# First attention: the subtraction of the row maximum moved from GpSimd to VectorE, with five neighbours moved to other places

## The chip, the core and the metric

The kernel runs on one core of one Trainium2 chip. The metric is the device time of one execution in microseconds (us); it is told as the median of three runs.

## The reference, cut to what matters

Sixteen images of 16 x 16 pixels with 128 channels go through three layers, each with a residual sum:

- `x = x + conv(group_norm(x))`: the first attention, windows of 8 x 8 pixels, 16 heads of 32, with a relative position bias and shift masks: `attn = softmax(q k^T * scale + bias + mask)`, `out = attn v`, then an output product;
- `t = t + attention(layer_norm(t))`: the second attention, in the kernel over the 256 tokens of an image, 8 heads of 16;
- `t = t + ffn(layer_norm(t))`: a router picks 2 of 8 experts for each token, and each expert is a gated two-layer net.

The change touches the first attention's softmax, which the kernel computes in explicit passes over scores in SBUF: bias added, maximum of each row, **maximum subtracted**, exponential, sum, reciprocal, product with the reciprocal. The change keeps these passes and what each computes.

## The kernel before, in words

The five engines run separate programs that meet at semaphores; the order of each program is written out by hand. After a prologue comes a loop of 24 iterations, `pipeline` (L366), in which iteration i works on nine images at nine stages of the chain at once (`LAGS`, L361; in the code X, G, A, M, Bm, T, R, L, K):

- X normalises image i+2 (GpSimd: `xns`, `xnl`), G makes its q, k, v for image i+1 (TensorE into `pG`, ScalarE evicts);
- **A** is the first attention of image i, in four units u = 0 to 3 of 128 x 512 scores (`pa`);
- **M** is image i-1: the first attention's output product (L1337, into `pM`), residual sum `t1` (VectorE L945), layer norm statistics (L949, L983, L986), the power -0.5 on GpSimd (`rs1`, L594), the normalised `tn1` (VectorE L1002), its transposes on TensorE (L1363), the split `t1h`/`t1l`, the q and k products of the second attention (L1184 to L1186 into `pM`), their evictions `kst` and `qst` (ScalarE L717, L721; low parts on VectorE L970, L972), and 12 DMAs on SP's queue that lay them out (L457, L461);
- **Bm** and **T** are the second attention of images i-2 and i-3: scores in `pSA`/`pSB` (L1240), their maximum `mxb` (VectorE L979), transposed scores (L1275), exponentials `ptb` (ScalarE L760);
- R, L, K are images i-4 to i-6: second layer norm, router, slots, and the scattering of token records to HBM by indirect DMA from GpSimd's queue (`depart`, `scatter`, L533 to L551).

Every engine runs through eight steps n = 0 to 7 per iteration, and at each step does its share of every stage in a fixed order; an instruction that waits holds everything behind it on its engine. What matters around the change:

- TensorE computes the scores of two units at a time at n = 0 and n = 4 (L1264): the even unit in `pSA`, the odd one in `pTA`. VectorE adds the bias into `pa` (L994, both units, at n = 0 and 4).
- VectorE takes the maximum `mxa` of unit n/2 at n = 0, 2, 4, 6 (L1017); GpSimd subtracts it at the same n (L623); ScalarE takes the exponential of unit (n-1)/2 at n = 1, 3, 5, 7 (L754); VectorE sums it (L1027) and takes the reciprocal `rca` (L1037); GpSimd multiplies (L631, "norm" below) at the same odd n. TensorE transposes the unit one step later (L1349, at n = 2, 4, 6 and the next n = 0), and ScalarE evicts it (`pta`, L777).
- At n = 2 TensorE's product L1337 waits for VectorE's `place` (L925) and `lg` (L899), which use the same bank `pM`.
- TensorE's L1184 for the key, query and value chunks (`pG`) waits until ScalarE has evicted the chunk before (k L687, q L692, v L737), because there is one bank for them.
- At n = 4 VectorE's order is: maximum of the second attention's head (L979), bias adds (L994), `tn1` (L1002), `tn2` (L1009), `mxa` (L1017). At n = 6 it is: `kst`, `qst` low parts (L970, L972), L979, `mxa`.
- GpSimd's order at n = 2 to 5 is: subtract u = 1 and a scatter (n = 2); `rs2` power L601, `mine` L605, two scatters, norm u = 1 (n = 3); `rs1` power L594, subtract u = 2, `xnl` L645, a scatter (n = 4); `t1b` L598, norm u = 2 (n = 5).

After the loop the experts' weights are loaded, tokens are gathered by expert, and the FFN runs (from about 540 us on in the trace); the change does not touch that part.

Of the kernel before, what the change touches and what calls it, by code (L numbers as in the profile page):

```python
# [11 lines left out]
WIN = 64  # L12
# [24 lines left out]
AU, BU = 4, 8  # L37
# [4 lines left out]
TB = 4  # L42
# [19 lines left out]
def wait(eng, sem, value):  # L62

    if value <= 0:
        return
    eng.wait_ge(sem, value)
# [60 lines left out]
def hybrid_kernel(nc, x_tok, x_ch, w0, wo0, bo0, pos, mask, ident_d, gmat_d, sel_d, iota_d,  # L127
# [5 lines left out]
    with ctx:  # L133
# [366 lines left out]
        def _(pool):  # L500
# [52 lines left out]
            def iteration(X, G, A, M, Bm, T, R, L, K):  # L553
# [30 lines left out]
                for n in range(8):  # L584
# [7 lines left out]
                    if n == 4 and M is not None:  # L592
                        pool.wait_ge(m_eps, M.j + 1)
                        pool.tensor_tensor(rs1[:, :], rs1[:, :], half[:, 0:2], ALU.pow).then_inc(m_pow, 1)  # L594
                    if n == 5 and M is not None:
                        pool.wait_ge(m_t, M.j + 1)
                        wait(pool, r_t, M.j - TB + 1)
                        pool.tensor_tensor(t1b[:, M.j % TB, :, :], t1[:, :, :], bo1s[:, :, :], ALU.add).then_inc(m_tb, 1)  # L598
# [13 lines left out]
                    if n == 3:  # L612
                        depart(K, n)
# [5 lines left out]
                    if A is not None and n % 2 == 0:  # L619

                        u = n // 2
                        pool.wait_ge(sa_max, A.j * AU + (u + 1))
                        pool.tensor_tensor(pa[:, u, :, :], pa[:, u, :, :],  # L623
                                           mxa[:, u % 2, :].unsqueeze(2).to_broadcast([128, 8, WIN]),
                                           ALU.subtract).then_inc(sa_sub, 1)
# [28 lines left out]
                    if n != 3:  # L654
                        depart(K, n)
# [186 lines left out]
        def _(v):  # L842
# [47 lines left out]
            def iteration(X, G, A, M, Bm, T, R, L, K):  # L890
                for n in range(8):
# [66 lines left out]
                    if T is not None and n == 7:  # L958
# [7 lines left out]
                                        rco[:, :, :].unsqueeze(3).to_broadcast([128, 2, H1, D1]), ALU.mult).then_inc(ot_nrm, 1)  # L966
                    if M is not None and n == 6:
# [6 lines left out]
                    if M is not None and n == 3:  # L974
                        v.wait_ge(m_st, M.j + 1)
                    if Bm is not None:
                        bank = (pSB, pSA)[n % 2]
                        v.wait_ge(sb_mm, Bm.j * BU + (n + 1))
                        v.tensor_reduce(mxb[:, Bm.par, n % 2, n // 2 * 2:n // 2 * 2 + 2], bank[:, :].rearrange("p (a k) -> p a k", a=2), AX.X,  # L979
                                        ALU.max, negate=True).then_inc(sb_max, 1)  # L980
# [577 lines left out]
```

## Time and profile before

| what | value |
|---|---|
| runs of the kernel before | 706.55, 712.59, 710.5 us; median 710.5 us |
| the profiled execution's own time | 709.77 us |
| its span, first to last instruction | 708.0 us |
| mean granted TensorE clock | 0.954 of full speed |
| busy: PE, PEld, DVE, ACT, POOL | 598.8, 479.6, 438.5, 410.4, 396.2 us |

PE is TensorE's products, PEld its weight loads (they overlap the products), DVE is VectorE, ACT is ScalarE, POOL is GpSimd, SP the engine that only issues DMAs here. "[0.83 <-POOL pa L631]" behind an instruction means that its engine sat idle for 0.83 us in front of it and that the last thing it waited for was GpSimd's instruction of line 631. The profiled execution is one of its own; its time stands 0.7 us under the median of the three runs.

### The profile page before, as it was taken

What the parts mean: (1) busy time and instruction counts of PE and PEld (TensorE: products, weight loads), DVE (VectorE), ACT (ScalarE), POOL (GpSimd) and SP (SyncE); (2) the same over time, 40 slices, a digit from 0 to 9 for tenths busy, and PEclk for the clock granted to TensorE, in tenths of its full rate; (3) what the DMA queues carried; (4) which work ended last, traced back from release to release, by engine and by line L of the source; (5) the groups of instructions that cost most, each with busy time, mean ns of one, the idle gap of its engine ahead of it and who ended that gap; (6) DMA issues with size and microseconds to landing.
All of it is one profiled execution on the core that took longest, in us unless ns stands there. A gap on an engine that the chain in (4) does not pass through costs nothing.

```text
span 708.0 us, 18292 instructions
## 1 busy us (share of the span) xinstructions
PE 598.8 (85%) x6460; PEld 479.6 (68%) x6460; DVE 438.5 (62%) x1325; ACT 410.4 (58%) x915; POOL 396.2 (56%) x503
## 2 busy tenths in 40 slices
PE   4877889999989899899899998988975799999910
PEld 3656667777767777677677776766655688888810
DVE  5534666767767677677776777765433365555625
ACT  2445576787676667766767677444411366666600
POOL 5665653454546576665665765642376066666643
PEclk9799999999999999999999999999996899999975
DMA  7100220231422414224133242243841122233237
GB/s 213 25 2 1 54 54 13 50 69 56 120 43 91 118 37 119 57 86 126 42 104 89 66 122 57 85 124 91 270 182 49 47 87 87 84 91 91 72 135 254
DMA packets 54511, 63.08 MB, mean 89 GB/s; under 512 B 12978, under 2 KB 47794, under 8 KB 53906
## 3 DMA queue, kind: packets, MB, share of 16 engines
q1 hardware_dynamic: 48294, 49.59, 25.3%
q0 software_dynamic: 4544, 9.38, 3.9%
q10 hardware_dynamic: 1584, 2.95, 1.2%
q8 instruction: 53, 0.87, 0.5%
q14 instruction: 36, 0.29, 0.1%
HBM read 35.74 MB, written 28.64 MB: 91 GB/s over the span
## 4 chain that ended last, share of the span: by engine, by line
PE 42%; POOL 17%; issue 15%; DVE 10%; ACT 7%; DMA 6%; SPq 2%; ACTq 0%; DVEq 0%; POOLq 0%
POOL slots L549 5%; POOL pa L623 4%; POOL pa L631 3%; PE pG L1192 3%; PE pSA L1264 3%; DMA slots<-sel_dram 2%; PE pSB L1438 2%; PE pTA L1438 2%; PE pTB L1438 2%; PE pSA L1438 2%; PE pTA L1349 2%; DVE pa L994 2%; PE pOA L1449 2%; PE pOB L1449 2%; PE pOB L1293 2%
## 5 line engine op out<-in xcount | busy, mean ns | idle before, releaser
L623 POOL TENSOR_TENSOR pa<-pa,mxa 128x512 f32<-128x512 f32 x64 | 66.7, 1042 | 110.9 <-DVE mxa L1017 110.8
L664 POOL DMA_INDIRECT ysl<-yo,dst x78 | 75.5, 968 | 59.7 <-DVE yo L1154 45.3
L631 POOL TENSOR_TENSOR pa<-pa,rca 128x512 f32<-128x512 f32 x64 | 67.0, 1047 | 63.5 <-DVE rca L1037 63.3
L760 ACT ACTIVATE ptb<-pTB 128x512 f32<-128x512 f32 x128 | 76.6, 599 | 43.1 <-PE pTB L1275 42.7
L549 POOL DMA_INDIRECT slots<-rec,slot x64 | 65.1, 1017 | 15.9 <-issue 13.2
L777 ACT ACTIVATE pta<-pTA 128x512 f32<-128x512 f32 x64 | 38.5, 602 | 56.1 <-PE pTA L1349 55.6
L1027 DVE TENSOR_REDUCE sma<-pa 128x8 f32<-128x512 f32 x64 | 43.8, 684 | 37.8 <-ACT pa L754 37.8
L754 ACT ACTIVATE pa<-pa 128x512 f32<-128x512 f32 x64 | 40.2, 628 | 42.2 <-POOL pa L623 41.9
L1349 PE MATMUL pTA<-ident,pa 128*128 128x128 f32 x256 | 40.3, 281 | 24.0 <-DVE pa L994 14.7
L979 DVE TENSOR_REDUCE mxb<-pSA 128x2 f32<-128x512 f32 x64 | 44.0, 688 | 25.1 <-PE pSA L1240 24.5
L1275 PE MATMUL pTB<-q,kbd 100*128 100x256 f32 x256 | 56.1, 301 | 0.1
L979 DVE TENSOR_REDUCE mxb<-pSB 128x2 f32<-128x512 f32 x64 | 44.0, 687 | 18.3 <-PE pSB L1240 16.2
L1184 PE MATMUL pG<-xnh,w0h 128*128 128x256 f32 x120 | 40.1, 334 | 13.8 <-ACT v L737 4.8
L1128 DVE COPY xs<-pG 128x256 f32<-128x256 f32 x39 | 16.6, 425 | 55.1 <-PE pG L1431 55.1
L1349 PEld LDWEIGHTS pTA<-ident,pa 128*128 128x128 f32 x256 | 28.0, 142 | 33.2 <-POOL pa L631 19.6
L737 ACT ACTIVATE v<-pG 64x256 f32<-64x256 f32 x120 | 45.3, 378 | 8.8 <-PE pG L1186 7.8
L1275 PEld LDWEIGHTS pTB<-q,kbd 100*128 100x128 f32 x256 | 42.3, 190 | 8.0 <-ACT q L780 2.7
L1314 PEld LDWEIGHTS pOA<-pta,v 128*64 128x64 f32 x1024 | 35.1, 137 | 17.7 <-issue 7.0
L1314 PE MATMUL pOA<-pta,v 128*64 128x64 f32 x1024 | 43.9, 228 | 1.7 <-ACT pta L777 1.1
L1017 DVE TENSOR_REDUCE mxa<-pa 128x8 f32<-128x512 f32 x64 | 43.2, 675 | 0.0
L807 ACT ACTIVATE ws<-fw 128x773 f32 x39 | 33.0, 848 | 17.1 <-issue 10.6
L1264 PEld LDWEIGHTS pSA<-k,q 32*64 32x64 f32 x1024 | 33.1, 135 | 11.7 <-issue 11.7
(227 smaller groups left out, 1738.3 us busy)
## 6 DMA issues: line engine op xcount, KB each, us to landing
slots<-sel_dram SPq DMA_DIRECT2D x16, 1040.0 KB
kbd<-kst SPq DMA_DIRECT2D x128, 48.0 KB, 2.2
q<-qst SPq DMA_DIRECT2D x64, 96.0 KB, 2.2
xt<-slots SPq DMA_DIRECT2D x39, 130.0 KB, 2.2
xch<-x_ch_dram SPq DMA_DIRECT2D x4, 512.0 KB, 5.8
xt<-x_tok_dram SPq DMA_DIRECT2D x16, 128.0 KB, 2.3
xch<-t SPq DMA_DIRECT2D x16, 128.0 KB, 4.6
fw<-f_dram SPq DMA_DIRECT2D x1, 2048.0 KB
```

The source lines that it names most:

```text
L549: pool.indirect_dma_start(slots, bass.IndirectOffsetOnAxis(ap=slot[:, J.j % RBUFS, k, s:s + 1], axis=0), rec[:, J.j % RBUFS, s, k, :], Non ...
L623: pool.tensor_tensor(pa[:, u, :, :], pa[:, u, :, :], mxa[:, u % 2, :].unsqueeze(2).to_broadcast([128, 8, WIN]), ALU.subtract).then_inc(sa_ ...
L631: pool.tensor_tensor(pa[:, u, :, :], pa[:, u, :, :], rca[:, b, :].unsqueeze(2).to_broadcast([128, 8, WIN]), ALU.mult).then_inc(sa_nrm, 1)
L664: pool.indirect_dma_start(ysl, bass.IndirectOffsetOnAxis(ap=dst[:, t % YB, n:n + 1], axis=0), yo[:, t % YB, n, :], None).then_inc(y_dma[t ...
L737: last = a.activation(v0[WIN * half_:WIN * half_ + WIN, J.par, 2 * pr + w, :, :, half_, :], projection(J, value_use(pr))[WIN * w:WIN * w + ...
L760: a.activation(ptb[:, h % PTBUFS, :, :], pTB[:, :].rearrange("p (a b) -> p a b", a=2), ACT.Exp).then_inc(st_exp, 1)
L979: v.tensor_reduce(mxb[:, Bm.par, n % 2, n // 2 * 2:n // 2 * 2 + 2], bank[:, :].rearrange("p (a k) -> p a k", a=2), AX.X, ALU.max, negate=T ...
L1264: mm = pe.matmul(bank[WIN * w:WIN * w + WIN, (pr * NCH + c) * WIN:(pr * NCH + c + 1) * WIN], q0[D0 * r:D0 * r + D0, A.par, c, t:t + WIN], ...
L1275: mm = pe.matmul(pTB[:, kc * TOK:(kc + 1) * TOK], kbd1[J.par][0:MROW + QUAD, h // 2, h % 2, kc * 128:(kc + 1) * 128], q1[0:MROW + QUAD, J. ...
L1314: mm = pe.matmul(pOA[WIN * jj:WIN * jj + WIN, w * WIN:(w + 1) * WIN], v0[:, J.par, w, jj, u, :, :].rearrange("p a d -> p (a d)"), pta[:, u ...
L1349: mm = pe.transpose(pTA[:, jj * 128:(jj + 1) * 128], pa[:, u, 2 * jj:2 * jj + 2, :].rearrange("p h k -> p (h k)"), ident[:, :])
L1438: mm = pe.matmul(bank[:, c * TS:(c + 1) * TS], ws[:, t % STG, w], xs[:, t % 2, :], start=True, stop=True)
```

## The change

On GpSimd: the four subtractions of an iteration are gone; the `rs1` power goes from the head of n = 4 to n = 3, before norm u = 1; the scatters of n = 3 go from before norm u = 1 to the end of the step; the `t1b` sum goes from before norm u = 2 to after it (n = 5). On VectorE: unit 0's and unit 2's maximum come right behind the bias adds at n = 0 and 4, in front of `tn1` and `tn2`, each followed by its subtraction; unit 1's and unit 3's come behind the reciprocal at n = 1 and 5 instead of at n = 2 and 6, each followed by its subtraction; at n = 6 the maximum of the second attention's head goes in front of the `kst` and `qst` low parts.

```diff
@@ -589,13 +589,6 @@
-                    if n == 4 and M is not None:
-                        pool.wait_ge(m_eps, M.j + 1)
-                        pool.tensor_tensor(rs1[:, :], rs1[:, :], half[:, 0:2], ALU.pow).then_inc(m_pow, 1)
-                    if n == 5 and M is not None:
-                        pool.wait_ge(m_t, M.j + 1)
-                        wait(pool, r_t, M.j - TB + 1)
-                        pool.tensor_tensor(t1b[:, M.j % TB, :, :], t1[:, :, :], bo1s[:, :, :], ALU.add).then_inc(m_tb, 1)
@@ -609,20 +602,14 @@
-                    if n == 3:
-                        depart(K, n)
+                    if n == 3 and M is not None:
+                        pool.wait_ge(m_eps, M.j + 1)
+                        pool.tensor_tensor(rs1[:, :], rs1[:, :], half[:, 0:2], ALU.pow).then_inc(m_pow, 1)
...
-                    if A is not None and n % 2 == 0:
-                        u = n // 2
-                        pool.wait_ge(sa_max, A.j * AU + (u + 1))
-                        pool.tensor_tensor(pa[:, u, :, :], pa[:, u, :, :],
-                                           mxa[:, u % 2, :].unsqueeze(2).to_broadcast([128, 8, WIN]),
-                                           ALU.subtract).then_inc(sa_sub, 1)
@@ -651,8 +638,11 @@
-                    if n != 3:
-                        depart(K, n)
+                    if n == 5 and M is not None:
+                        pool.wait_ge(m_t, M.j + 1)
+                        wait(pool, r_t, M.j - TB + 1)
+                        pool.tensor_tensor(t1b[:, M.j % TB, :, :], t1[:, :, :], bo1s[:, :, :], ALU.add).then_inc(m_tb, 1)
+                    depart(K, n)
@@ -964,13 +954,6 @@
-                    if M is not None and n == 6:
-                        v.wait_ge(m_qhi, M.j + 1)
-                        v.scalar_tensor_tensor(kst1[:, 1, :], pM[:, 0:TOK], bk1s[:, 0:1], kst1[:, 0, :].bitcast(f32),
-                                               ALU.add, ALU.subtract).then_inc(m_klo, 1)
-                        v.scalar_tensor_tensor(qst1[:, 2, :], pM[:, TOK:2 * TOK], bq1x[:, 0:1], qst1[:, 0, :].bitcast(f32),
-                                               ALU.add, ALU.subtract).then_inc(m_qlo, 1)
@@ -978,6 +961,13 @@
+                    if M is not None and n == 6:
+                        v.wait_ge(m_qhi, M.j + 1)
+                        v.scalar_tensor_tensor(kst1[:, 1, :], pM[:, 0:TOK], bk1s[:, 0:1], kst1[:, 0, :].bitcast(f32),
+                                               ALU.add, ALU.subtract).then_inc(m_klo, 1)
+                        v.scalar_tensor_tensor(qst1[:, 2, :], pM[:, TOK:2 * TOK], bq1x[:, 0:1], qst1[:, 0, :].bitcast(f32),
+                                               ALU.add, ALU.subtract).then_inc(m_qlo, 1)
@@ -995,6 +985,16 @@
+                    if A is not None and n % 4 == 0:
+                        u = n // 2
+                        b = u % 2
+                        v.wait_ge(sa_add, A.j * AU + (u + 1))
+                        wait(v, sa_sub, A.j * AU + (u - 1))
+                        v.tensor_reduce(mxa[:, b, :], pa[:, u, :, :], AX.X, ALU.max).then_inc(sa_max, 1)
+                        v.wait_ge(sa_max, A.j * AU + (u + 1))
+                        v.tensor_tensor(pa[:, u, :, :], pa[:, u, :, :],
+                                        mxa[:, b, :].unsqueeze(2).to_broadcast([128, 8, WIN]),
+                                        ALU.subtract).then_inc(sa_sub, 1)
@@ -1009,12 +1009,6 @@
-                    if A is not None and n % 2 == 0:
-                        u = n // 2
-                        b = u % 2
-                        v.wait_ge(sa_add, A.j * AU + (u + 1))
-                        wait(v, sa_sub, A.j * AU + (u - 1))
-                        v.tensor_reduce(mxa[:, b, :], pa[:, u, :, :], AX.X, ALU.max).then_inc(sa_max, 1)
@@ -1035,6 +1029,16 @@
+                    if A is not None and n % 4 == 1:
+                        u = n // 2 + 1
+                        b = u % 2
+                        v.wait_ge(sa_add, A.j * AU + (u + 1))
+                        wait(v, sa_sub, A.j * AU + (u - 1))
+                        v.tensor_reduce(mxa[:, b, :], pa[:, u, :, :], AX.X, ALU.max).then_inc(sa_max, 1)
+                        v.wait_ge(sa_max, A.j * AU + (u + 1))
+                        v.tensor_tensor(pa[:, u, :, :], pa[:, u, :, :],
+                                        mxa[:, b, :].unsqueeze(2).to_broadcast([128, 8, WIN]),
+                                        ALU.subtract).then_inc(sa_sub, 1)
```

## Rows read from the trace of the kernel before

**Rows 1.** The page's costliest groups: line, engine, operation, busy us, mean ns, idle before.
```profile
L623 POOL TENSOR_TENSOR pa<-pa,mxa 128x512 f32<-128x512 f32 x64 | 66.7, 1042 | 110.9 <-DVE mxa L1017 110.8
```

**Rows 2.** Busy time by engine in iteration 10: length, then each engine, clock, DMA.
```profile
296.60:324.90 28.30, 26.20 (x359) 20.80 (x353) 20.72 (x62) 20.16 (x48) 18.37 (x25) 1.00 0.31 86
```

**Rows 3.** TensorE's waits in iteration 10: total us, times, longest.
```profile
PE pTA L1349 <- POOL pa L631: 0.8, 1, 0.8
PE pTA L1349 <- DVE pa L994: 0.8, 2, 0.5
PE pG L1184 <- ACT q L692: 0.3, 1, 0.3
```

**Rows 4.** TensorE's waits in iteration 4, 126.5 to 153.7 us.
```profile
PE pG L1184 <- ACT q L692: 0.8, 2, 0.5
PE pOB L1375 <- DVE on L965: 0.3, 1, 0.3
```

**Rows 5.** Timeline of VectorE at the kernel's end: start, us, instruction.
```profile
689.75 0.68 DVE L1174 TENSOR_TENSOR yc<-yc,xch 128x512 f32<-128x512 f32 x1
690.47 1.63 DVE L1177 TENSOR_TENSOR yc<-yc 128x512 f32<-128x512 f32 x1
```

**Rows 6.** Timeline of GpSimd in the same stretch.
```profile
689.92 1.63 POOL L668 TENSOR_TENSOR yc<-yc 128x512 f32<-128x512 f32 x1 [7.21 <-DVE yc L1174]
```

**Rows 7.** VectorE's sums of L884, at 13 to 15 us: ns min/median/max.
```profile
L884 DVE TENSOR_TENSOR bias<-posr,t2f x16: 163/168/720, 13.0 to 14.8; 128x8 f32<-128x8 f32 x16
```

**Rows 8.** Timeline of GpSimd in the prologue.
```profile
13.91 1.80 POOL L557 MEMSET v<- 128x2048 f32 x1
```

**Rows 9.** Timeline of VectorE, iteration 11, steps 4 and 2.
```profile
331.16 0.17 DVE L925 TENSOR_TENSOR place<-pM,ebase 128x16 f32<-128x16 f32 x1
...
339.35 0.68 DVE L994 TENSOR_TENSOR pa<-pTA,bias 128x512 f32<-128x512 f32 x1
340.57 0.60 DVE L1002 TENSOR_SCALAR tn<-t,mv,rs 128x128 f32<-128x128 f32 x2 [0.54 <-POOL rs L594]
```

**Rows 10.** Timeline of VectorE, iteration 4, step 4.
```profile
140.68 0.60 DVE L1002 TENSOR_SCALAR tn<-t,mv,rs 128x128 f32<-128x128 f32 x2
```

**Rows 11.** Timeline of TensorE, iteration 4, step 4.
```profile
142.00 0.44 PE L1363 MATMUL pM<-ident,tn 128*128 128x128 f32 x2
```

**Rows 12.** Timeline of TensorE, iteration 11, steps 2 and 4, and the next step 0.
```profile
331.68 1.95 PE L1337 MATMUL pM<-wo0s,o 128*128 128x128 f32 x16
...
341.26 0.44 PE L1363 MATMUL pM<-ident,tn 128*128 128x128 f32 x2
...
351.75 0.40 PE L1240 MATMUL pSB<-kbd,q 96*128 96x512 f32 x1
```

**Rows 13.** Timeline of GpSimd, iteration 11, step 1.
```profile
329.97 1.04 POOL L631 TENSOR_TENSOR pa<-pa,rca 128x512 f32<-128x512 f32 x1 [0.73 <-DVE rca L1037]
```

**Rows 14.** Timeline of ScalarE, iteration 11, step 6.
```profile
345.45 0.71 ACT L717 ACTIVATE kst<-pM,bk1s 128x512 fp32r<-128x512 f32 x1
...
347.33 0.44 ACT L692 ACTIVATE q<-pG 128x256 f32<-128x256 f32 x1
```

**Rows 15.** SP's queue in iteration 11, and L461's landing times over the whole span.
```profile
348.56 0.59 SPq L461 DMA_DIRECT2D q<-qst  x1
...
DMA to landing us min/median/max: 2.2/2.2/3.4
```

**Rows 16.** Timeline of VectorE in iteration 1, step 0.
```profile
48.56 0.67 DVE L1017 TENSOR_REDUCE mxa<-pa 128x8 f32<-128x512 f32 x1
```

**Rows 17.** Timeline of GpSimd in iteration 1, steps 0 and 1.
```profile
53.33 1.04 POOL L623 TENSOR_TENSOR pa<-pa,mxa 128x512 f32<-128x512 f32 x1
...
56.07 1.04 POOL L631 TENSOR_TENSOR pa<-pa,rca 128x512 f32<-128x512 f32 x1 [0.44 <-DVE rca L1037]
```

**Rows 18.** Timeline of TensorE in iteration 1, steps 1 and 2.
```profile
55.35 0.39 PE L1184 MATMUL pG<-xnh,w0h 128*128 128x256 f32 x1 [4.14 <-ACT k L687]
...
59.23 0.60 PE L1349 MATMUL pTA<-ident,pa 128*128 128x128 f32 x4
```

## The prediction, made before the changed kernel ran

> **What bounds the kernel now.** I read the busy time by stretch first, then TensorE's waits, then the timelines of one iteration. The loop is settled from iteration 10 on: the same instruction returns every 28.3 us. In it TensorE is busy 26.2 of 28.3 us, VectorE 20.7, ScalarE 20.2, GpSimd 18.4 [rows 2]. So an iteration can lose at most the 2.1 us in which TensorE waits, and only what ends one of those waits counts. They are: 0.8 for the product with the reciprocal on GpSimd (norm u = 2, at step 6), 0.8 in two pieces for the bias adds, 0.3 for ScalarE's q eviction at step 7 [rows 3], the rest in pieces of 0.2. The 110.9 us that GpSimd idles before its subtractions [rows 1] cost nothing by themselves. The adds' waits stay: TensorE cannot transpose into `pTA` before they have emptied it. So 1.1 us are within reach in a late iteration. In iterations 3 to 6, where nothing is scattered yet, the norm's wait is missing; within reach are the q waits, two in 0.8, and 0.3 for `on1` [rows 4].
>
> **The price of the subtraction on VectorE.** It is not in the trace. Nearest rows: a sum of the same shape from two SBUF operands takes 0.68 us [rows 5], the bias add from PSUM 0.68 [rows 9]; GpSimd's takes 1.04 [rows 1]. I take 0.68, with 0.60 from start to start (340.57 is the add's 339.35 plus 0.60, 0.08 of its tail and the 0.54 wait [rows 9]). The other end is 1.63, which the same shape takes at the kernel's end where GpSimd works on two SBUF operands: GpSimd's L668 came 0.51 us before L1174 had ended and took 1.63 instead of 1.04; VectorE's L1177 then waited about 0.95 for it [rows 5, 6]. Each waits for all of the other. One of the 16 sums of L884 shows it as well, 720 ns against 168; the others ran at 168, most of them beside a memset of GpSimd, which holds nothing up [rows 7, 8].
>
> The Trainium skill (GPSIMD Engine Reference, "Elementwise — side-by-side cycle accounting") puts a two-input sum on GpSimd at 1.96 times VectorE's time; from 1.04 that is an estimate of 0.53, and the sum below would be some 2 us lower by it. The trace's ratio is 1.53, and it is what I use.
>
> **Step 4, the dear place.** Maximum and subtraction now stand in front of `tn1`. In iteration 11 the maximum can start at 339.95, is done 0.68 later, the subtraction starts at about 340.66 and `tn1` at 341.26, not at 340.57 [rows 9]: +0.7 us, although the power that `tn1` waited for is now early. TensorE transposes `tn1` at 341.26, just as the first half lands [rows 12], so the 0.7 goes to TensorE whole. In iteration 4 `tn1` ran right behind the add, 140.68 to 141.28 [rows 10], and TensorE took it up 0.7 us later, at 142.00 [rows 11]; there the delay is 1.3 us and TensorE loses 0.65. So **+0.65 to +0.7 in every iteration from 3 on**. If GpSimd's `xnl` sum happens to hold the operands, up to 0.5 more.
>
> **Step 1 to 2.** The reciprocal releases both norm u = 0 on GpSimd (329.97 to 331.01 [rows 13]) and, on VectorE, the maximum and subtraction of u = 1. The maximum is done at about 330.5; the subtraction then waits for the norm until 331.0, as L1177 does [rows 5, 6], and ends at 331.56. Behind it stand `lg` and `place`; `place` would end at 331.81, not 331.33 [rows 9], and TensorE's L1337, which starts at 331.68 [rows 12], goes back by **0.3** in the iterations from 6 on. Without that collision: nothing. `t2` and `mxb` behind it have room.
>
> **Step 5 to 7.** Norm u = 2 no longer stands behind the subtraction, the scatters and `t1b`; the exponential of u = 2 follows `t1h` at once, so the norm ends over 1 us before TensorE comes to it: **-0.8** [rows 3]. The exponential of u = 3 is no longer the thing that ScalarE waits for at step 7, so q is evicted early: **-0.3** [rows 3, 4]; in iterations 3 to 6 the 0.3 for `on1` goes too, because no maximum stands before it [rows 4]. But `kst` and `qst` follow TensorE's product, which steps 2 and 4 have put back by 1.0. ScalarE then ran without a gap from 345.45 to the q of 347.33 [rows 14]; that q ends about 0.9 later, and TensorE's key chunk of step 7, which waits for it, loses **0.4 to 0.5**. That wait stands in iteration 4 already (the other half of the 0.8 [rows 4]).
>
> **The queues.** SP issues `kst`'s and `qst`'s DMAs behind VectorE's low parts. `qst`'s first is issued at 348.56 and lands in 2.2 us, at 350.8; TensorE wants it at 351.75 less its weight load [rows 12, 15]. Put back by 0.9 it lands at 351.65, just in time. I take nothing; with a landing of 3.4 it is 1.2. The head maximum in front of the low parts is ready before `qst`: nothing. The scatters behind norm u = 1 and `t1b` behind norm u = 2 feed stages that are iterations away: nothing, and GpSimd gains four times 1.04 us, which covers them. The power at step 3 waits for `m_eps`; behind it stands only norm u = 1, released later.
>
> **Late iteration:** +0.7 + 0.3 + 0.45 - 0.8 - 0.3 = +0.3, of which some 0.2 may come back, because the gap before the transposes of step 6 is wider than the idle time counted for it (an estimate); +0.1, times nine (7 to 15): +1. **Iterations 3 to 6:** +0.65 - 0.3 - 0.3, about +0.1 each: +0.4.
>
> **The fill.** In iteration 1 the maximum is there at 49.23 [rows 16], but GpSimd, with the set-up of constants ahead in its queue, subtracts at 53.33 [rows 17]; the exponential, ScalarE's k behind it and TensorE's chunk wait for that, 4.14 us [rows 18]. On VectorE the subtraction can run at 49.3 beside the memsets [rows 7, 8]. What is late next is norm u = 0, still behind the set-up and two `xns` passes: without the 1.04 and the 0.44 wait it starts at about 54.6, not 56.07 [rows 17], and ends at 55.7; TensorE's transposes come then instead of at 59.23 [rows 18]: **-3.5**. Iterations 0 and 2, which lose the same wait in small and gain the one for `tn1`, give some 0.5 together (an estimate). In the drain the moved power can give about the 0.54 that `tn1` waits for it in the loop [rows 9], once; I count nothing.
>
> **Sum:** -4 + 0.4 + 1 = -2.6. On the profiled execution's 709.8 that is 707.2; the median of the runs stands 0.7 higher. I forecast **707.5**.
>
> **Rivals.**
> *A trade of waits (forecast), 0.58:* above.
> *Faster, 0.24:* the two new waits that I derived at one remove, `place` at step 2 and q at step 7, do not appear (the subtraction gets its operands before the norm, or ScalarE catches up). Then nine late iterations lose 0.3 + 0.45 less each, -7: **700.5**. For it: the fill's gain is certain in kind and GpSimd is relieved of 66.7 us [rows 1]. Against it: the wait of L1177, and the same q wait in iteration 4 [rows 4 to 6].
> *Slower, 0.18:* the low parts come so late that `qst`'s DMA holds TensorE at step 0. It decides once they come over 1 us later than now. At the longest landing, 1.2 us in 14 iterations, 17 us: **724**; with half of it 716. For it: 0.1 us of room by my own working. Against it: the usual landing of 2.2 [rows 15].
> That the change doesn't do what it says, a subtraction that always waits for GpSimd, adds at most 0.5 at step 4 in ten iterations, +5: 712.5, in the range.
>
> **How the numbers follow.** 1% is 7 us, about what a measurement can tell from no change. The forecast's own spread (0.53 to 1.63 for a subtraction apart, the terms at one remove) is 702 to 713. Faster by over 1% means under 703.4: the faster rival's better part and a little of the forecast's, 0.23. Slower means over 717.6: the worse part of the DMA rival, 0.13. Within: 0.64. The range, 699 to 717, takes in the faster rival and half of the slower.
>
> **What would show it.** Right: L1017 and the subtraction of 0.68 between L994 and L1002; TensorE waiting 0.6 to 0.7 for `tn1` at L1363; the wait for L631 at step 6 gone; the 4.14 of iteration 1 gone; a settled period of 28.2 to 28.6. Wrong: a period under 27.9, no wait at L1363, or waits of TensorE for `q<-qst` in most iterations.

## The result, and the profile after

The changed kernel takes 715.96 us (median of 20 runs) against 708.9 us (20 runs) before: a ratio of 1.0100, 95% interval 1.0072 to 1.0129. It is 1% slower; the forecast was a little faster, so the sign was wrong. The profile that came with these runs is of a slow execution (724.7 us), so the rows below are from a second series of the same kernel: 718.06 against 708.99 us, 1.0118 (1.0075 to 1.016), its profiled span 717.6 us, before 708.0.

I compare by iterations; iteration i begins with the first bias add of image i, and ends where that of image i+1 begins.

| | to iteration 3 | 3 and 4 | 5 to 9 | 10 to 14 | rest | span |
|---|---|---|---|---|---|---|
| before, us | 99.67 | 54.16 | 142.87 | 141.43 | 269.9 | 708.0 |
| after, us | 98.78 | 54.93 | 150.69 | 142.19 | 271.0 | 717.6 |
| difference | -0.9 | +0.8 | **+7.8** | +0.8 | +1.1 | +9.6 |

**Where it went as forecast.** Iteration 10 of the changed kernel, in the columns of [rows 2] (length, then PE, PEld, VectorE, ScalarE, GpSimd, clock, DMA):
```profile
304.40:332.86 28.46, 26.21 (x353) 20.70 (x353) 24.01 (x66) 19.97 (x48) 15.05 (x20) 1.00 0.31 85
```
VectorE has 3.3 us more to do, GpSimd 3.3 less, and the period is 0.17 longer (28.29 before). All waits of TensorE of 0.15 us or more in iteration 11 (timeline: start, length, instruction, idle time before it and what ended it):
```profile
334.30 0.63 PE L1353 MATMUL pTA<-ident,pa 128*128 128x128 f32 x4 [0.36 <-DVE pa L984]
348.40 0.63 PE L1353 MATMUL pTA<-ident,pa 128*128 128x128 f32 x4 [0.53 <-DVE pa L984]
350.25 0.44 PE L1367 MATMUL pM<-ident,tn 128*128 128x128 f32 x2 [0.69 <-DVE tn L1002]
356.71 0.39 PE L1188 MATMUL pG<-xnh,w0h 128*128 128x256 f32 x1 [0.45 <-ACT q L682]
```
Against [rows 3], the 0.8 for the norm at step 6 and the 0.3 for q are gone; a 0.69 for `tn1`, and a 0.45 for q in front of a key chunk, have come. VectorE in step 4 of the same iteration, against [rows 9]:
```profile
347.57 0.68 DVE L984 TENSOR_TENSOR pa<-pTA,bias 128x512 f32<-128x512 f32 x1
348.17 0.68 DVE L993 TENSOR_REDUCE mxa<-pa 128x8 f32<-128x512 f32 x1
348.88 0.79 DVE L995 TENSOR_TENSOR pa<-pa,mxa 128x512 f32<-128x512 f32 x1
349.60 0.59 DVE L1002 TENSOR_SCALAR tn<-t,mv,rs 128x128 f32<-128x128 f32 x2
```
The two instructions between the add and `tn1` are the delay. All 64 subtractions, by line (busy us, mean ns, idle before):
```profile
L1039 DVE TENSOR_TENSOR pa<-pa,mxa 128x512 f32<-128x512 f32 x32 | 33.9, 1059 | 1.1
L995 DVE TENSOR_TENSOR pa<-pa,mxa 128x512 f32<-128x512 f32 x32 | 22.8, 713 | 1.1
```
Those of u = 0 and 2 cost 0.71; those of u = 1 and 3 run into the norm that the same reciprocal releases on GpSimd and take 1.06 (in 31 of 32 cases they end 0.55 us behind it; the one without a norm beside it took 0.69).

**Where it did not.** TensorE's waits in iterations 5 to 9 (total us, times, longest), first before, then after:
```profile
PE pTA L1349 <- DVE pa L994: 4.8, 10, 0.6
PE pTA L1349 <- POOL pa L631: 2.5, 3, 0.8
PE pG L1184 <- ACT q L692: 2.3, 7, 0.5
PE pOB L1375 <- DVE on L965: 0.6, 2, 0.3
PE pG L1184 <- ACT v L737: 0.5, 3, 0.2
```
```profile
PE pTA L1353 <- DVE pa L984: 5.6, 10, 0.7
PE pSB L1244 <- DMA q<-qst: 3.7, 4, 1.0
PE pM L1367 <- DVE tn L1002: 3.2, 5, 0.7
PE pG L1188 <- ACT q L682: 2.3, 5, 0.5
PE pM L1341 <- DVE lg L889: 0.4, 1, 0.4
```
Waits of 10.7 us have become 15.2. The 2.5 for the norm are gone; 3.2 for `tn1`, which was forecast, and 3.7 for the copy of the second attention's queries at step 0 are new. The same five iterations as one row each, before and after:
```profile
153.83:296.70 142.87, 131.88 (x1757) 104.10 (x1757) 102.47 (x305) 100.67 (x236) 82.53 (x110) 0.99 0.29 82
```
```profile
153.71:304.40 150.69, 135.14 (x1757) 106.20 (x1757) 119.58 (x326) 100.71 (x236) 65.91 (x91) 0.95 0.28 78
```
TensorE ran the same 1757 matmuls and needed 3.3 us more for them, at a mean clock of 0.95 and not 0.99. So the 7.8 us are 4.5 of waits and 3.3 of a lower clock. The clock falls behind such a wait; iteration 8's, and 5 us stretches around it:
```profile
272.17 0.50 PE L1244 MATMUL pSB<-kbd,q 96*128 96x512 f32 x1 [1.04 <-DMA q<-qst]
```
```profile
265.00:270.00 5.00, 4.55 (x47) 3.99 (x46) 4.83 (x12) 4.06 (x9) 1.52 (x3) 1.00 0.13 25
270.00:275.00 5.00, 3.54 (x77) 2.52 (x76) 2.07 (x5) 3.18 (x9) 3.74 (x7) 0.94 0.48 96
275.00:280.00 5.00, 4.77 (x21) 3.56 (x22) 3.38 (x8) 2.90 (x6) 0.38 (x1) 0.50 0.61 173
```
0.50 is the lower of the two levels, 1.2 GHz. Not every such wait is followed by a dip, and the runs of one kernel differ in it. Of the seventeen traces, the ten with a wait of 0.3 us or more for the copies in iterations 4 to 14 all have an iteration there with a mean clock of 0.95 or less; of the seven others two have one (the kernel before, in iteration 8, and run 3).

**The margin.** SP's issue of the first query copy and TensorE's step 0, in iteration 11 after (against [rows 12, 15]):
```profile
357.44 0.60 SPq L461 DMA_DIRECT2D q<-qst  x1
```
```profile
359.75 0.40 PE L1244 MATMUL pSB<-kbd,q 96*128 96x512 f32 x1
```
From issue to use it is 2.31 us; before it was 3.19 (348.56 to 351.75). A copy that lands in time needs about 2.25 (run 5 below, where TensorE waits for it in every settled iteration). So the change took the margin from 0.9 to 0.05 us. In iteration 8 the same distance is 3.51; of the 1.2 more, 1.04 is the wait shown above.

### The profile page after: what moved, and what is told of

The parts are those of the page before. It is cut to its first block, busy times and chain, and to the rows that moved or that the text cites. A ratio compares the mean times of both kernels' runs of the same rounds, so it can differ in the third digit from the quotient of the medians.

```text
span 722.5 us, 18292 instructions
## 1 busy us (share of the span) xinstructions
PE 609.2 (84%) x6460; PEld 487.9 (68%) x6460; DVE 487.1 (67%) x1389; ACT 412.0 (57%) x915; POOL 341.3 (47%) x439
## 4 chain that ended last, share of the span: by engine, by line
PE 59%; DVE 13%; issue 9%; DMA 7%; SPq 4%; ACT 4%; POOL 3%; ACTq 0%; DVEq 0%; POOLq 0%
PE pM L1341 4%; PE pOA L1318 4%; PE pOB L1297 4%; PE pSA L1268 4%; DMA q<-qst 3%; PE pG L1196 3%; DVE pa L984 3%; PE pTA L1353 3%; PE pTB L1279 3%; PE pG L1188 2%; PE pSB L1442 2%; PE pTB L1442 2%; PE pTA L1442 2%; PE pSA L1442 2%; PE pOA L1453 2%
## 5 line engine op out<-in xcount | busy, mean ns | idle before, releaser
L549 POOL DMA_INDIRECT slots<-rec,slot x64 | 68.8, 1075 | 16.2 <-issue 13.7
L1353 PE MATMUL pTA<-ident,pa 128*128 128x128 f32 x256 | 42.1, 290 | 20.3 <-DVE pa L984 16.7
L1021 DVE TENSOR_REDUCE sma<-pa 128x8 f32<-128x512 f32 x64 | 43.5, 680 | 10.9 <-ACT pa L744 10.7
L1318 PEld LDWEIGHTS pOA<-pta,v 128*64 128x64 f32 x1024 | 37.0, 144 | 17.8 <-issue 7.9
L1353 PEld LDWEIGHTS pTA<-ident,pa 128*128 128x128 f32 x256 | 30.2, 148 | 27.2 <-issue 22.7
L1318 PE MATMUL pOA<-pta,v 128*64 128x64 f32 x1024 | 46.0, 235 | 1.5 <-ACT pta L767 1.1
L1268 PE MATMUL pTA<-k,q 32*64 32x64 f32 x1024 | 37.3, 221 | 0.0
L1268 PE MATMUL pSA<-k,q 32*64 32x64 f32 x1024 | 37.0, 221 | 0.0
```

The costliest lines, as they stand in the source:

```text
L549: pool.indirect_dma_start(slots, bass.IndirectOffsetOnAxis(ap=slot[:, J.j % RBUFS, k, s:s + 1], axis=0), rec[:, J.j % RBUFS, s, k, :], Non ...
L1268: mm = pe.matmul(bank[WIN * w:WIN * w + WIN, (pr * NCH + c) * WIN:(pr * NCH + c + 1) * WIN], q0[D0 * r:D0 * r + D0, A.par, c, t:t + WIN], ...
L1318: mm = pe.matmul(pOA[WIN * jj:WIN * jj + WIN, w * WIN:(w + 1) * WIN], v0[:, J.par, w, jj, u, :, :].rearrange("p a d -> p (a d)"), pta[:, u ...
L1353: mm = pe.transpose(pTA[:, jj * 128:(jj + 1) * 128], pa[:, u, 2 * jj:2 * jj + 2, :].rearrange("p h k -> p (h k)"), ident[:, :])
```

## The experiments

Settled: mean period of iterations 10 to 13. Distance: from the first query copy's issue to the score that uses it, in a settled iteration. Excess: iterations 5 to 9 less five settled periods. Each ratio is to executions of the kernel before on the same chip; runs 1 to 8, 9 to 12, 13 and 14, and 15 were on four different chips, so between these groups ratios compare better than medians. Settled, distance and excess are each from one trace.

| run | median us | ratio to before, 95% | settled | distance | excess |
|---|---|---|---|---|---|
| before | 708 to 711 | 1 | 28.29 | 3.19 | 1.4 |
| 1 changed, again | 718.1 | 1.0118, 1.0075 to 1.0160 | 28.45 | 2.31 | 8.4 |
| 2 tn1 first | 718.9 | 1.0134, 1.0098 to 1.0169 | 28.83 | 2.32 | 7.8 |
| 3 subtraction alone | 711.6 | 1.0041, 1.0012 to 1.0071 | 28.57 | 3.40 | 1.0 |
| 4 moves alone | 705.1 | 0.9931, 0.9897 to 0.9964 | 27.81 | 2.59 | 3.1 |
| 5 tn1 and tn2 first | 716.2 | 1.0097, 1.0064 to 1.0130 | 28.52 | 2.25 | 3.5 |
| 6 as 5, low parts first | 705.1 | 0.9948, 0.9916 to 0.9979 | 27.94 | 2.27 | 4.1 |
| 7 as 4, low parts first | 706.3 | 0.9982, 0.9957 to 1.0006 | 28.38 | 3.19 | -0.3 |
| 8 as 6, GpSimd's old order | 707.0 | 0.9974, 0.9946 to 1.0003 | 27.90 | 2.32 | 5.0 |
| 9 changed, turned | 704.7 | 0.9945, 0.9923 to 0.9966 | 28.20 | 3.51 | 0.7 |
| 10 as 6, turned | **689.7** | **0.9740, 0.9705 to 0.9775** | 27.51 | 3.25 | 0.1 |
| 11 as 4, subtraction on VectorE in the fill | 700.9 | 0.9880, 0.9842 to 0.9917 | 27.77 | 2.60 | 8.4 |
| 12 changed, TensorE awake | 717.8 | 1.0104, 1.0061 to 1.0148 | 28.43 | 2.31 | 5.1 |
| 13 before, turned | 705.8 | 0.9959, 0.9931 to 0.9986 | 28.06 | 4.37 | -0.6 |
| 14 as 11, turned | 692.4 | 0.9787, 0.9756 to 0.9818 | 27.55 | 3.79 | -0.9 |
| 15 changed, fetch shifted | 721.5 | 1.0171, 1.0107 to 1.0235 | | | |

(Settled in run 8: iterations 10 to 12; in run 12: 12 to 14. In run 15 late copies fall among 10 to 13, see there.)

**Run 1, the changed kernel again** (no edit).

> The changed kernel once more, for a second trace of it and its time on the same chip as the next three. Theory A (the maximum and the subtraction in front of the layer norm's scaling tn1 make TensorE wait in step 4 of every iteration and make the copies of the second attention's queries late for the next step 0): 714 to 718 us, with TensorE waits for tn1 of 0.6 to 0.7 us in every iteration from 3 on and for the query copies of 0.4 to 1.1 us in some of iterations 2 to 8. Theory B (the time is lost to TensorE's granted clock in the fill, iterations 2 to 4): the same time, but the start of the first attention's bias additions of iteration 5 is already 4 us or more later than before, and the iterations from 5 on are as long as before.

Theory A's waits are there, of `tn1` in every iteration and of the copies in 1, 2 and 5 to 8. Iteration 5 starts at 153.71, before at 153.83: theory B fell. The clock does cost something, but mostly in iterations 7 and 9 (0.89 each), less in 2 and 3 (0.96 and 0.91).

**Run 2, `tn1` in front.**
```diff
+ if M is not None and n == 4:
+     wait(v, m_T, M.j)
+     v.wait_ge(m_pow, M.j + 1)
...
  if A is not None and n % 4 == 0:
      u = n // 2
...
- if M is not None and n == 4:
-     wait(v, m_T, M.j)
-     v.wait_ge(m_pow, M.j + 1)
...
```


> The changed kernel with one thing put back: in step 4 the layer norm's scaling tn1 stands in front of the first attention's maximum and subtraction on VectorE, not behind them. Theory A (those 1.3 us in front of tn1 are the loss): the wait for tn1 falls from 0.7 to below 0.1 us in every iteration, the waits for the query copies go, and the time is 704 to 710 us. Theory B (clock in the fill): the fill's two waits for norm stay, 712 to 717 us. Theory C (VectorE simply has 3 us more to do in every iteration): 713 to 717 us, the wait moves to the transposes of the first attention's probabilities.

A failed as I had put it. The wait for `tn1` is gone, but TensorE waits 0.95 us for `tn2` a little later, and 0.5 to 1.4 for the copies.

**Run 3, the subtraction alone.**
```diff
  if A is not None and n % 2 == 0:
...
      v.tensor_reduce(mxa[:, b, :], pa[:, u, :, :], AX.X, ALU.max).then_inc(sa_max, 1)
+     v.wait_ge(sa_max, A.j * AU + (u + 1))
+     v.tensor_tensor(pa[:, u, :, :], pa[:, u, :, :],
+                     mxa[:, b, :].unsqueeze(2).to_broadcast([128, 8, WIN]),
+                     ALU.subtract).then_inc(sa_sub, 1)
...
- if A is not None and n % 2 == 0:
-
-     u = n // 2
-     pool.wait_ge(sa_max, A.j * AU + (u + 1))
...
```


> The kernel before with the subtraction alone on VectorE, right behind each maximum in its old place (steps 0, 2, 4, 6, behind tn1 and tn2); GpSimd's order, the score maximum and the maxima stay as before. Theory A: no wait for tn1, the wait for the norm is shorter than before by the subtraction's time on GpSimd; 702 to 708 us. Theory C (VectorE's load): 713 to 718 us. Theory D (it is the other moves that cost): 702 to 708 us too, and the next kernel slower.

Between the theories. It has the fill's gain (iteration 3 starts at 94.0, not 99.7) and no wait for the copies, but 1.01 us for `on1` in each iteration, with u = 3's two instructions in step 6, ahead of it.

**Run 4, the moves alone**: the maximum is back in its old place on VectorE (first part of the diff), the subtraction on GpSimd (last lines).
```diff
- if A is not None and n % 4 == 0:
...
- if A is not None and n % 4 == 1:
...
+ if A is not None and n % 2 == 0:
+     u = n // 2
+     b = u % 2
...
+     v.tensor_reduce(mxa[:, b, :], pa[:, u, :, :], AX.X, ALU.max).then_inc(sa_max, 1)
...
+ if A is not None and n % 2 == 0:
+
+     u = n // 2
+     pool.wait_ge(sa_max, A.j * AU + (u + 1))
...
```


> The changed kernel with the subtraction left on GpSimd and the maxima in their old places: only the power, the scatters, the sum t1b and step 6's score maximum stand where the change puts them. Theory A and C: 706 to 711 us, as before. Theory D (the moves of the power, the scatters, t1b and the score maximum cost what was lost): 713 to 718 us, with the query copies behind the score maximum 0.9 us later and TensorE waiting for them in step 0.

D fell: the moves are a gain. With the power and the scatters out of its way, the norm is no longer waited for (-0.5 in the period). The margin shrinks with it, to 0.3 us, and the copies are waited for in four of iterations 5 to 9.

**Run 5, `tn1` and `tn2` in front.**
```diff
+ if M is not None and n == 4:
+     wait(v, m_T, M.j)
+     v.wait_ge(m_pow, M.j + 1)
...
+ if R is not None and n == 4:
+     wait(v, r_two, R.j - 1)
+     v.wait_ge(r_pow, R.j + 1)
...
  if A is not None and n % 4 == 0:
      u = n // 2
...
- if M is not None and n == 4:
-     wait(v, m_T, M.j)
-     v.wait_ge(m_pow, M.j + 1)
...
- if R is not None and n == 4:
-     wait(v, r_two, R.j - 1)
-     v.wait_ge(r_pow, R.j + 1)
...
```


> The changed kernel with the first maximum and subtraction of step 4 put behind both scalings, tn1 and tn2 (the run with tn1 alone in front moved the wait to tn2). Theory A2 (whatever stands behind those 1.3 us in step 4 and feeds TensorE is late; there is a slot behind both): neither tn waits, a settled iteration falls from 28.45 to 27.7 to 27.9 us, 703 to 709 us, and the waits for the query copies in iterations 5 to 9 stay in part. Theory C (VectorE's load): the wait comes up a third time, at on1 or at the probabilities' transposes, and a settled iteration stays above 28.3 us, 711 us or more.

Neither `tn` waits now, and TensorE waits 0.6 us for the query copies in each settled iteration. Theory C's period and time came (28.52, 716.2), its place did not. The period had two bounds: TensorE's own work with its waits, and the chain from `tn1` over `kst`, `qst` and their copies to the next step 0. A wait taken out of the first only shows the second.

**Run 6, the low parts first too**: the edit of run 5, and
```diff
+ if M is not None and n == 6:
+
+     v.wait_ge(m_qhi, M.j + 1)
+     v.scalar_tensor_tensor(kst1[:, 1, :], pM[:, 0:TOK], bk1s[:, 0:1], kst1[:, 0, :].bitcast(f32),
...
  if Bm is not None:
      bank = (pSB, pSA)[n % 2]
...
- if M is not None and n == 6:
-
-     v.wait_ge(m_qhi, M.j + 1)
-     v.scalar_tensor_tensor(kst1[:, 1, :], pM[:, 0:TOK], bk1s[:, 0:1], kst1[:, 0, :].bitcast(f32),
...
```


> As the run before it, and in step 6 the two low parts kst and qst stand in front of the score maximum again. Theory A2 with E (the low parts behind the score maximum make the query copies late): no wait for the query copies in iterations 2 to 9, 698 to 704 us. Rival F (the query copies are late because the scatters moved, or because their landing takes longer in these iterations): within 2 us of the run before it, with the same waits.

705.1 us is 11 less than in run 5, so F fell as a whole, and just outside E's 698 to 704. E holds where the chain is the bound: the settled period falls by 0.6, and its wait for the copies is gone. In iterations 5 to 9 the copies are still waited for, 0.3 to 0.8: there, as F says, the landing takes longer (see run 15).

**Run 7, the same order in run 4**: its edit, and
```diff
+ if M is not None and n == 6:
+
+     v.wait_ge(m_qhi, M.j + 1)
+     v.scalar_tensor_tensor(kst1[:, 1, :], pM[:, 0:TOK], bk1s[:, 0:1], kst1[:, 0, :].bitcast(f32),
...
  if Bm is not None:
      bank = (pSB, pSA)[n % 2]
...
- if M is not None and n == 6:
-
-     v.wait_ge(m_qhi, M.j + 1)
-     v.scalar_tensor_tensor(kst1[:, 1, :], pM[:, 0:TOK], bk1s[:, 0:1], kst1[:, 0, :].bitcast(f32),
...
```


> The kernel with the moves alone (subtraction on GpSimd) and the low parts in front of the score maximum again. Theory E: the query copies' waits of iterations 5 to 9 (1.9 us in all) go, on1's wait of 0.3 us comes back; 701 to 705 us. Rival F: the waits stay, 704 to 707 us.

No wait for the copies, as E said, but 706.3 us, outside E's 701 to 705: q (0.30) and `on1` (0.29) are waited for in each iteration instead, and a settled one is 0.57 longer.

**Run 8, GpSimd's old order**: VectorE as in run 6, and on GpSimd the power, t1b and step 3's scatters in front of the norm again.
```diff
+ if n == 4 and M is not None:
+     pool.wait_ge(m_eps, M.j + 1)
...
+ if n == 5 and M is not None:
+     pool.wait_ge(m_t, M.j + 1)
...
+ if n == 3:
+     depart(K, n)
...
+ if n != 3:
+     depart(K, n)
- depart(K, n)
```


> VectorE as in the run with both scalings and the low parts first, but GpSimd's power, scatters and t1b at their places of before (the subtraction is on VectorE). If the power's place in step 3 is a gain of its own: tn1 is up to 0.5 us later than in that run and a settled iteration 0.2 to 0.5 us longer, 702 to 708 us. If the subtraction's leaving GpSimd already gives all of it: within 2 us of that run.

With the subtraction gone from GpSimd its order is worth nothing that can be seen in a settled iteration (27.90 against 27.94), and the copies are waited for as in run 6. The norm is not waited for here either.

**Run 9, the turn.** At step 0 the second attention's first score goes behind the first attention's scores, which gives the copies 1.2 us more (3.51 against 2.31).
```diff
- if Bm is not None:
+ if Bm is not None and (n > 0 or A is None):
...
  if A is not None and n % 4 == 0:
...
+ if Bm is not None and A is not None and n == 0:
+
+     if n % 2 == 0:
+         pe.wait_ge(kq_dma[Bm.par][n // 2], Bm.half * 48 + 48)
...
```
(on VectorE the score's maximum goes behind the first subtraction in the same way).

> The changed kernel with one order turned round: at step 0 the second attention's first score pSB stands behind the first attention's scores on TensorE (its maximum behind the first subtraction on VectorE), so the query copies have 0.9 to 1.0 us longer to land. Theory S (the change leaves the copies about 0.05 us between landing and TensorE's step 0 where the kernel before left 0.9, so each landing that takes longer in iterations 1, 2 and 5 to 9 becomes a wait, and most of the loss is there): the waits for the query copies of 0.4 to 1.2 us are gone or below 0.2, iterations 5 to 9 together take 143 to 146 us and not 150.7, a settled iteration stays at 28.3 to 28.5, 706 to 711 us. Rival W (VectorE's work and the wait for tn1 in every iteration are the loss): 714 us or more.

Theory S held, by more than I had put: iterations 5 to 9 take 141.7 us (143 to 146 expected), a settled one 28.20 (28.3 to 28.5). Nothing else of the change is undone, TensorE still waits 0.58 to 0.69 for `tn1` in each iteration, and the kernel takes 704.65 us where the changed one took 715.96 and 718.06. TensorE's waits in iterations 5 to 9, and those iterations as a row:
```profile
PE pM L1384 <- DVE tn L1007: 3.1, 5, 0.7
PE pTA L1370 <- DVE pa L984: 2.8, 5, 0.7
PE pG L1193 <- ACT q L682: 2.3, 5, 0.5
PE pSA L1273 <- issue: 0.8, 1, 0.8
PE pM L1358 <- DVE lg L889: 0.4, 1, 0.4
```
```profile
149.42:291.10 141.68, 130.75 (x1757) 102.93 (x1757) 118.35 (x325) 100.97 (x236) 65.56 (x90) 1.00 0.30 82
```
The copies' wait is gone and the clock is full. Iteration 3 starts at 96.13: the forecast's 3.5 us of the fill are there.

**Run 10, the turn in run 6** (edits of runs 6 and 9).

> The same turn in the kernel that had both scalings and the low parts first (705.1 us). Theory S: no waits for the query copies, iterations 5 to 9 take 139 to 141 us together (143.8 without the turn), a settled iteration 27.3 to 27.9; 697 to 702 us. Rival: TensorE's other waits take the time back, 703 to 706 us.

Better than expected (iterations 5 to 9 take 137.7 us), and 2.6% faster than the kernel before: the fastest version found. All waits of TensorE of 0.15 us or more in its iteration 11 (timeline):
```profile
317.33 2.02 PE L1358 MATMUL pM<-wo0s,o 128*128 128x128 f32 x16 [0.28 <-DVE place L915]
325.91 0.63 PE L1370 MATMUL pTA<-ident,pa 128*128 128x128 f32 x4 [0.53 <-DVE pa L984]
333.40 0.39 PE L1193 MATMUL pG<-xnh,w0h 128*128 128x256 f32 x1 [0.45 <-ACT q L682]
```
The first is the `place` that the prediction derived for step 2, at 0.28.

**Run 11, the subtraction on VectorE in the fill alone**: the edit of run 4, and on VectorE and GpSimd
```diff
      v.tensor_reduce(mxa[:, b, :], pa[:, u, :, :], AX.X, ALU.max).then_inc(sa_max, 1)
+     if A.j <= 1:
+         v.wait_ge(sa_max, A.j * AU + (u + 1))
+         v.tensor_tensor(pa[:, u, :, :], pa[:, u, :, :],
+                         mxa[:, b, :].unsqueeze(2).to_broadcast([128, 8, WIN]),
+                         ALU.subtract).then_inc(sa_sub, 1)
...
- if A is not None and n % 2 == 0:
+ if A is not None and A.j > 1 and n % 2 == 0:
```


> The kernel with the moves alone (705.1 us), and the subtraction on VectorE in the first two images alone, where GpSimd's memsets hold it; from the third image on it is GpSimd's. If the subtraction's move is worth something in the fill alone: TensorE's wait of 4.1 us for the keys' evacuation in iteration 1 is gone, iteration 3 starts at 94 to 96 us and not 100.1, 699 to 702 us. Rival: the gain is given back before iteration 5 by the next waits or by a lower clock, 703 to 706 us.

As expected: iteration 3 starts at 95.11, 4.95 us sooner than in run 4, the median is 4.2 lower. The copies are still waited for (0.60, 0.30 and 0.91 in iterations 6 to 8), and iteration 7 takes 33.9 us at a clock of 0.80.

**Run 12, TensorE kept awake at the wait.**
```diff
+ if n == 0 and A is not None and Bm.j in (0, 1, 4, 5, 6, 7, 8):
+     wait(pe, sb_max, Bm.j * BU - 1)
+     keep_awake(pSB, 4)
  if n % 2 == 0:
      pe.wait_ge(kq_dma[Bm.par][n // 2], Bm.half * 48 + 48)
```


> The changed kernel with four matmuls of 128x512 without use in front of step 0's wait for the query copies, in the iterations that waited there (for second-attention images 0, 1 and 4 to 8): TensorE is busy in most of that wait. If the dips of the granted clock behind these waits come from TensorE's idle time: no 5 us stretch below 0.8 between 205 and 290 us, iterations 5 to 9 together below 148 us, 710 to 714 us. If the dips have another cause: they stay, 715 to 719 us.

The dips between 205 and 290 us are gone and iterations 5 to 9 take 147.29, at clock 1.00, as the first theory said; the time did not fall with them. The four matmuls hold TensorE as long as the wait did, iterations 9 and 10 came to wait for the copies (0.47, 0.77), 10 and 11 took 29.45 and 29.28 (11 at a clock of 0.94), and iteration 3 starts at 102.20, 3.4 later than in run 1. In this one trace, filling TensorE's idle time at the wait takes the dips away, and most of the loss remains, now in part as the four matmuls' own time.

**Run 13, the turn in the kernel before** (edit of run 9, VectorE's maximum behind `mxa`).

> The kernel before, its subtraction on GpSimd and all else as it was, with the turn alone: step 0's first score behind the first attention's scores on TensorE and its maximum on VectorE behind the bias additions and the first maximum. Theory S (the turn pays because the change used up the copies' margin; the kernel before has 0.9 us of it): no wait to remove but the 0.3 us at the probabilities' first transposes, a settled iteration 28.0 to 28.3 us, 703 to 708 us. Rival T (the turn is a gain of its own and the margin has no part in it): 697 us or less, the same 11 us that the changed kernel gained by it.

The control: the turn is worth 2 us to it, and 11 to 13 to the changed kernel (715.96 and 718.06 to 704.65). What it gives a settled iteration is nearly the same in both (28.29 to 28.06 here, 28.45 to 28.20 there); the rest is the copies' waits and what followed them. Rival T fell.

**Run 14, the turn in run 11** (edits of runs 9 and 11).

> The moves alone with the subtraction on VectorE in the first two images alone, and the turn. Theory S: iterations 5 to 9 take 138 to 140 us together and not 147.3, no wait for the query copies, a settled iteration 27.3 to 27.8; 690 to 696 us. If the subtraction on VectorE in every image is what made the fastest kernel so fast (689.7 us): 3 us or more slower than that; if it is the turn and the fill: within 3 us of it.

It is 2.7 us behind run 10 by the medians and 3.3 by the ratios, so the two branches are not told apart. Iterations 5 to 9 take 136.8 us, and the settled periods are nearly equal (27.55 and 27.51). So with the margin there the subtraction on VectorE need not cost a settled iteration anything; as the two kernels also differ in the places of the maxima and the low parts, what the subtraction's place alone is worth is not shown.

**Run 15, TensorE's instruction stream shifted.** Eight traces without the turn (the changed kernel's two, and runs 2, 4, 5, 6, 8, 11) were compared in the copies of iterations 4 to 14, 3.7 us from the first issue (a key copy's, 1.3 us ahead of the first query copy's). Runs 3, 7 and 12 and the kernel before were left out; their distance is wider, from the kernel's order or from run 12's matmuls. q8 is one of two DMA queues that the profile calls instruction queues. Where a packet of q8 lay among the copies, 33 times, TensorE waited 31 times; where none did, 55 times, it waited 8 times, 6 of them in run 5, whose copies are late anyway.

The landing itself shows it more sharply, in all seventeen traces and all sixteen iterations. Of 256 first query copies whose landing is known, 124 had no packet of either instruction queue among them and landed in 2.17 to 2.27 us. The 80 with a packet of q8 took 2.21 to 3.94 (74 of them over 2.6), the 52 with a packet of the other queue, q14, alone 2.16 to 2.88 (5 over 2.6).
```diff
  keep_awake(pSB, 6)
+ for _ in range(64):
+     pe.matmul(pSB[0:64, 0:64], w0h[0:32, 0:64], w0h[0:32, 0:64], start=True, stop=True)
```


> The changed kernel with 64 small matmuls without use (32 rows, 64x64) before the loop, some 11 us in, where TensorE waits for GpSimd. They add 128 instructions to TensorE's stream, half of what a 16 KB packet of its instruction queue holds by the traces' count (53 packets for some 13,000 instructions). Theory Q (the query copies land late when such a packet falls among them; where it falls drifts by a few instructions in an iteration): the waits of 0.4 to 1.0 us for the query copies leave iterations 5 to 8 and turn up some four or five iterations off (9 to 13, or before 5), each with a packet of that queue among the copies; 712 to 720 us. Rival: the landing is late in iterations 5 to 8 for what else these iterations do (the first scatters, the stages that come in); then the waits stay in 5 to 8.

The waits left iterations 5 to 8 and stand in 3 and 4 and 10 to 12 (0.64 to 1.08 us), with a q8 packet among the copies each time. Queues and landings of this run in iteration 12, then in iteration 8 (queue: packets, MB, share; issue: count, KB each, median us to landing):
```profile
q8 instruction: 1, 0.02, 1.7%
...
q<-qst SPq DMA_DIRECT2D x1, 96.0 KB, 3.5
```
```profile
q1 hardware_dynamic: 298, 0.24, 34.6%
issues: line engine op xcount, KB each, median us to landing
kbd<-kst SPq DMA_DIRECT2D x4, 48.0 KB, 2.2
q<-qst SPq DMA_DIRECT2D x2, 96.0 KB, 2.2
```
In iteration 8, q1, the copies' own queue, is the only one. Theory Q's places held; its time did not (721.5 us, 712 to 720 expected). The 64 matmuls took 7.0 us and put the loop's start back by 2.7; what else made it slower, no run shows.

## Why the prediction was wrong, by its steps

**The queues: the step that failed.** The text had the copies landing "just in time. I take nothing", and 1.2 for a late one. The geometry was right (0.1 us of room by its working, 0.05 measured); the size, zero, was wrong. It was mis-sized because [rows 15] was read as a usual 2.2 with a rare 3.4. The long landings come in a row, where instruction packets fall among the copies; the kernel before had them too, 3.4 us in iterations 7 and 8, and its margin hid all but 0.1 us of each (distance 3.46). The copies of its iteration 8, in the form used for run 15:
```profile
q8 instruction: 1, 0.02, 1.8%
...
q<-qst SPq DMA_DIRECT2D x1, 96.0 KB, 3.4
```
Measured: 3.7 us of waits and 3.3 of clock in iterations 5 to 9, and 0.87 and 1.15 of waits in iterations 1 and 2. (The first of these two copies landed in 2.19 and was only issued late; the second took 2.83, with a packet of q14 among the copies.) Runs 9 and 13 show that this is the loss. The slower rival had the mechanism and the place; 0.18 was too little for a margin that my own sum had used up. That its 716 is the measured time, inside the stated range, is luck: it had 0.6 us in each of 14 iterations, and no clock.

**Step 4** was right: 0.65 to 0.7 forecast, 0.58 to 0.69 measured; so was its effect on what follows, `kst` at 21.50 us after the iteration's first add and not 20.47. Run 2 shows what the text left out: `tn2` stands behind it.

**The price** was right in the open places (0.71 for 0.68) and in the collision at u = 1; u = 3 collides in the same way (1.06), which the text did not have. The 0.53 worked out from the ratio of the Trainium skill ("GPSIMD Engine Reference", "Elementwise — side-by-side cycle accounting") did not come: GpSimd's 1.04 against 0.71 is 1.46, not 1.96.

**Step 1 to 2:** TensorE's L1341 starts 6.97 us after the iteration's first add, not 6.70: the 0.3 forecast. As a wait for `place` it is 0.13 here and 0.28 in run 10.

**Steps 5 to 7** were right: the norm's 0.8 gone, 0.45 for q, no wait for `on1`. Run 4 corrects the cause: the norm's wait goes with the power's and the scatters' move alone, the subtraction need not leave GpSimd for it. Run 8 shows the reverse: with the subtraction gone, the moves are not needed for it.

**Late iteration:** +0.1 forecast, +0.17 measured.

**The fill:** -3.5 to -4 forecast; iteration 3 starts 0.9 earlier. GpSimd's hold on ScalarE's k (4.14 us) is gone, and the norm came a little sooner than worked out, its transposes at 55.07 (55.7 forecast) after 2.41 of wait; then `tn1` (1.11, 0.59) and the copies (0.87, 1.15) took most of it back. Without the copies' waits, in run 9, it is -3.5. The 0.9 is of one execution: in run 12, whose edit acts only from the end of iteration 1 on, iteration 1 already starts 1.2 later.

**Iterations 3 to 6:** +0.1 each forecast; 3 lost 0.9 at a clock of 0.91, 4 gained 0.1, and 5 and 6 lost 1.5 and 1.4, of which 0.75 and 0.91 are waits for the copies.

## What to carry to other kernels

A transfer that lands just in time is a cost, not a zero: before an edit that makes the consumer earlier or the producer later, write down the distance from issue to use and compare it with the longest landing, and look at where in the run the long ones lie. When a wait is removed and the period stays, look for a second chain that closes over the iteration; here it went through VectorE, SP's queue and a copy, and turning round two independent products on TensorE gave it 1.0 to 1.2 us for nothing. Judge a move by both of its effects: the same four subtractions on VectorE were a loss of 1%, or part of a gain of 2.6%, by what stood behind them.

## What the runs showed of the hardware

One packet of the instruction queue q8 (53 in the span, 0.87 MB, so about 16 KB each) among the second attention's copies that SP issues puts the landing of the first query copy from 2.2 to as much as 3.9 us (3.94 in run 8). That q8 is TensorE's is taken from run 15, where a shift of TensorE's stream moved the packets. A packet of q14 (7 KB on the mean) goes with up to 2.9 us; whose queue it is, no run shows. The Trainium skill ("Runtime: NRT & Kernel Launch", "Instruction fetch mechanics") says that each engine streams its instructions in 16 KiB blocks by its own DMA queue and that crossing a block is mostly hidden. The size of q8's packets agrees. Their cost was not hidden here, and it fell on the data copies beside them: 0.4 to 1.0 us of TensorE's wait each in the changed kernel. Which resource packets and copies share, no run here shows.
